# Cross-attention and expert FFN in one kernel: values laid out by partition, and the first batch's last scores, softmax and first values by halves of the queries

## The reference

```python
n = layernorm(x)                             # (8, 224, 2048)
a = einsum('bqd,bkd->bqk', n, ctx)           # scores against 750 context rows
x = x + einsum('bqk,bkd->bqd', softmax(a), ctx)
h = layernorm(x)
base = einsum('bsi,oi->bso', h, base_w) + base_b
hidden = einsum('bsi,ri->bsr', h, A)         # 64 wide
p = softmax(einsum('bsi,ei->bse', h, router_w))   # 16 experts, the best two kept
x = x + base + 0.5 * einsum('bse,bsr,eor->bso', combine(p), hidden, B)
```

## Time and profile before

| | us |
|---|---|
| median of 3 runs (1350.43 to 1354.08) | 1351.94 |
| the profiled execution, its own time | 1354.39 |
| its span, first to last instruction | 1352.6 |
| PE busy in the span | 1327.3 |
| DVE busy | 974.7 |
| ACT busy | 601.2 |
| mean granted clock of PE, share of full | 0.996 |

### The profile page before, as it was taken

How to read it: one execution, slowest core, us unless ns; L and a number is a source line. 1 busy time by engine, 2 the same in 40 slices (tenths; PEclk the granted TensorE clock), 3 DMA queues, 4 the chain that set the end, 5 groups by cost and what they waited for, 6 DMA issues and landing times.

```text
span 1352.6 us, 16784 instructions
## 1 busy us (share of the span) xinstructions
PE 1327.3 (98%) x6543; PEld 1081.0 (80%) x6543; DVE 974.7 (72%) x1254; ACT 601.2 (44%) x768; POOL 322.5 (24%) x229
## 2 busy tenths in 40 slices
PE   7799999999999999999999999999999999999998
PEld 5578788887878788887888888888788888888887
DVE  5698888889798888879475467777677555465554
ACT  3356554645546464546321367877686211111110
POOL 0003012130302112120615723354442111111110
PEclk9899999999999999999999999999999999999999
DMA  9976968878796977769657598999995977878775
GB/s 326 315 258 215 294 242 242 269 251 271 227 304 212 287 259 248 246 227 194 201 161 211 176 296 288 321 324 310 315 250 192 322 255 242 281 250 263 253 260 164
DMA packets 159359, 345.67 MB, mean 256 GB/s; under 512 B 51696, under 2 KB 68080, under 8 KB 145520
## 3 DMA queue, kind: packets, MB, share of 16 engines
q1 hardware_dynamic: 140688, 277.06, 64.5%
q0 software_dynamic: 10528, 52.85, 12.6%
q10 hardware_dynamic: 8064, 14.68, 3.1%
HBM read 260.87 MB, written 99.41 MB: 266 GB/s over the span
## 4 chain that ended last, share of the span: by engine, by line
PE 75%; DVE 12%; DMA 5%; ACT 3%; POOL 3%; issue 2%; SPq 0%; DVEq 0%; POOLq 0%; ACTq 0%
PE scores L937 12%; PE scores L939 12%; PE scores L938 12%; PE scores L906 6%; PE scores L908 6%; PE scores L907 6%; PE scores L789 4%; PE scores L791 3%; PE scores L790 3%; DVE ctxT_l L1287 3%; PE work L973 2%; PE work L974 2%; DMA y_scratch<-y_out,yrow_i 2%; DVE raw_l L1297 2%; POOL hs_scratch L1830 2%
## 5 line engine op out<-in xcount | busy, mean ns | idle before, releaser
L937 PE MATMUL scores<-w_h,a_h 128*128 128x512 f32 x896 | 352.0, 393 | 0.0
L939 PE MATMUL scores<-w_h,a_l 128*128 128x512 f32 x896 | 350.9, 392 | 0.0
L938 PE MATMUL scores<-w_l,a_h 128*128 128x512 f32 x896 | 350.6, 391 | 0.0
L1159 ACT ACTIVATE a_h<-a_in 128x512 fp32r<-128x512 f32 x148 | 83.6, 622 | 313.4 <-DMA a_in<-xT_scratch 211.3
L939 PEld LDWEIGHTS scores<-w_h,a_l 128*128 128x128 f32 x896 | 168.4, 188 | 37.5
L937 PEld LDWEIGHTS scores<-w_h,a_h 128*128 128x128 f32 x896 | 168.3, 188 | 37.5 <-DVE w_l L1584 0.3
L938 PEld LDWEIGHTS scores<-w_l,a_h 128*128 128x128 f32 x896 | 168.5, 188 | 37.1
L1593 DVE TENSOR_TENSOR a_l<-a_in,a_h 128x512 fp32r<-128x512 f32 x148 | 106.0, 763 | 115.3 <-ACT a_h L1159 111.8
L789 PE MATMUL scores<-ctxT_h,nT_h 128*112 128x494 f32 (+1 forms) x512 | 174.3, 340 | 7.8 <-DVE nT_l L1485 7.2
L1067 ACT ACTIVATE val_h<-raw_in 128x512 fp32r<-128x512 f32 x192 | 120.2, 629 | 127.6 <-PE scores L908 127.6
L791 PE MATMUL scores<-ctxT_h,nT_l 128*112 128x494 f32 (+1 forms) x512 | 171.5, 335 | 0.0
(11 more groups left out here) (168 smaller groups left out, 1936.6 us busy)
## 6 DMA issues: line engine op xcount, KB each, us to landing
ctxT_in<-in_ctxT_dram SPq DMA_DIRECT2D x63, 750.0 KB, 4.7
raw_in<-in_ctx_dram SPq DMA_DIRECT2D x32, 1280.0 KB
a_in<-xT_scratch SPq DMA_DIRECT2D x37, 1024.0 KB
w_in<-in_wT_dram SPq DMA_DIRECT2D x32, 512.0 KB, 6.7
y_add<-y_scratch SPq DMA_DIRECT2D x56, 256.0 KB, 6.2
late_y<-y_scratch SPq DMA_DIRECT2D x56, 256.0 KB, 6.0
nT_in<-in_xT_dram SPq DMA_DIRECT2D x7, 1792.0 KB, 10.1
res<-x_scratch SPq DMA_DIRECT2D x42, 256.0 KB
```

Of the source, the lines that this page charges most:

```text
L937: pe.matmul(o, ah, wh, start=(k == 0), stop=False)
L938: pe.matmul(o, ah, wl, start=False, stop=False)
L939: last = pe.matmul(o, al, wh, start=False, stop=(k == KD - 1))
```

## The change

Four things are edited together. (1) The host hands over the values as (batch, chunk, 125, 6, 512) and the kernel loads a chunk with one transfer of 125 partitions with 12 KB each; a tile is 125 rows, six of them make 750, and the last, shorter tile and the padding of `prob` are gone. (2) In batch 0, raw 1 is issued right behind raw 0, raw 2 behind `ctxT` 6, raw 3 behind `ctxT` 7. (3) In batch 0, the last two steps of the scores are reordered so that half 0 ends first; its maximum, exponentials, transposes and split come before those of half 1, and the first four value products run by halves. (4) The PSUM sides of batch 0 are swapped for that, batch 1 begins its scores with the other half, and DVE takes the first two statistics of batch 1's rows before the value products.

```diff
 def load_raw(b, c):
-    cols = slice(c * BANK, (c + 1) * BANK)
-    sp.dma_start(raw_in[:, c, 0:FULL, :],
-                 ctx[b, 0:FULL * P, cols].rearrange("(t p) d -> p t d", p=P)).then_inc(raw_loaded[c], 16)
-    sp.dma_start(raw_in[0:REST, c, FULL, :], ctx[b, FULL * P:LK, cols]).then_inc(raw_loaded[c], 16)
+    sp.dma_start(raw_in[0:KT, c, :, :], ctx[b, c]).then_inc(raw_loaded[c], 16)
...
-                    if first and j == LR + 1:
-                        load_raw(0, 1)
+                    if first and j == NPC - 2:
+                        load_raw(0, 2)
...
                     if first:
-                        load_raw(0, 2)
+                        load_raw(0, 3)
                         sp.dma_start(ar_in[:, :, :], arT).then_inc(ar_loaded, 16)
-                        load_raw(0, 3)
                         load_row(1)
...
             load_raw(0, 0)
+            load_raw(0, 1)
             one(0, "first")
...
+    def side_of(b, c):
+        return (c + 1) % 2 if b > 0 else c % 2
...
                 if stage == "first":
+                    k = KD - 2 * CP
+                    pe.wait_ge(first_ready, NPC - 1)
+                    pe.wait_ge(ctx_ready, b * NPC + NPC - 1)
+                    products(k, 0)
+                    products(k + 1, 0)
+                    products(k, 1)
                     pe.wait_ge(first_ready, NPC)
+                    pe.wait_ge(ctx_ready, b * NPC + NPC)
+                    products(k + 2, 0)
+                    products(k + 3, 0).then_inc(scores_done, 1)
+                    products(k + 1, 1).then_inc(score_step, 1)
+                    products(k + 2, 1)
+                    exps_T(stage, b, 0)
+                    products(k + 3, 1).then_inc(scores_done, 1)
+                    return
...
             def outputs_of(stage, b):
 
+                if stage == "first":
+                    pe.wait_ge(drained, job_no(stage, b, "eT", 0) + 1)
+                    for e in range(NR):
+                        if e == NR - 1:
+                            exps_T(stage, b, 1)
+                        pe.wait_ge(val_ready, b * (CH * NT) + e + 1)
+                        value_products(b, e, 0)
                 pe.wait_ge(drained, job_no(stage, b, "eT", NQ - 1) + 1)
-                for e in range(CH * NT):
+                if stage == "first":
+                    for e in range(NR):
+                        value_products(b, e, 1).then_inc(val_used, 1)
+                for e in range(NR if stage == "first" else 0, CH * NT):
...
                 row_max(b, 0)
                 if old:
                     x2T_low(2)
+                else:
+                    exps_low(0)
                 row_max(b, 1)
...
                 if old:
                     hidden_out(stage, b)
+                else:
+                    row_stats(1, 0, 2)
                 for e in range(NR, CH * NT):
                     value_low(b, e)
...
     laid["ctxT"] = ctx.transpose(0, 2, 1).reshape(nb, d // 256, 2, 128, lk).transpose(0, 1, 3, 2, 4)
+    laid["ctx_4096"] = ctx.reshape(nb, -(-lk // 128), -1, d // 512, 512).transpose(0, 3, 2, 1, 4)
```

More of the change, by code:

```diff
@@ L72, in xattn_ffn_kernel @@
     NB, LQ, D = x.shape
-    LK = ctx.shape[1]
+    LK = ctxT.shape[-1]
     E, R = bT.shape[0], bT.shape[1]
@@ L792, in products @@
                     return last
-                for j in range(NPC - 1):
+                for j in range(NPC - 1 if stage != "first" else NPC - 2):
                     if stage != "first" and j in X2T_BEFORE:
@@ L806, in scores_of @@
                     by_block = j or stage == "first"
-                    for k, q in itertools.product(ks, (1, 0)) if by_block else [(k, q) for q in (1, 0) for k in ks]:
+                    halves_first = (0, 1) if b == 1 else (1, 0)
+                    for k, q in itertools.product(ks, (1, 0)) if by_block else [(k, q) for q in halves_first for k in ks]:
                         if stage == "first" and (k, q) == (1, 1):
@@ L875, in hidden_back @@
                 last.then_inc(filled, 1)
[L877 to L886, removed]
@@ L888, in outputs_of, with exps_T @@
-            def outputs_of(stage, b):
+            def exps_T(stage, b, q):
+                pe.wait_ge(exp_done, b * NQ + q + 1)
+                take(job_no(stage, b, "eT", q))
+                slot = slot_of(stage, "eT", q)
+                for t in range(NT):
+                    at = (t // 3) * BANK + (t % 3) * QT
+                    last = pe.transpose(work[0:KT, slot, at:at + QT],
+                                        prob[:, q, t * KT:(t + 1) * KT], ident[0:QT, 0:QT])
+                last.then_inc(filled, 1)
@@ new lines, in value_products @@
+            def value_products(b, e, q):
+                c, t = e // NT, e % NT
+                out = scores[0:QT, side_of(b, c), q * BANK:(q + 1) * BANK]
+                eh, el = eT_h[0:KT, q, t, :], eT_l[0:KT, q, t, :]
+                vh, vl = val_h[0:KT, e % NR, :], raw[0:KT, c, t, :]
+                pe.matmul(out, eh, vh, start=(t == 0), stop=False)
+                pe.matmul(out, eh, vl, start=False, stop=False)
+                last = pe.matmul(out, el, vh, start=False, stop=(t == NT - 1))
+                return last
@@ L901, in outputs_of @@
                     for q in range(NQ):
[L902 to L908, removed]
+                        last = value_products(b, e, q)
                     last.then_inc(val_used, 1)
@@ L916, in one @@
                     hidden_of(stage, b, 0, HID_EARLY)
-                exps_T(stage, b)
+                if stage != "first":
+                    for q in range(NQ):
+                        exps_T(stage, b, q)
                 if stage != "first":
@@ L1037, in high @@
                 act.wait_ge(filled, job_no(stage, b, name, n) + 1)
-                src = place(stage, name, n).rearrange("p (k c) -> p k c", k=cols)[:, :, 0:width]
+                rows = out.shape[0]
+                src = place(stage, name, n)[0:rows, :].rearrange("p (k c) -> p k c", k=cols)[:, :, 0:width]
                 act.activation(out, src, ACT.Copy).then_inc(high_done, 1)
@@ L1119, in one @@
                     high(stage, b, "x2T", NX - 1, four_blocks(nT_h, NX - 1), 2, 2 * LQ)
+                three = lambda q: eT_h[0:KT, q, :, :].rearrange("p (k i) c -> p k (i c)", k=2)
+                if stage == "first":
+                    high(stage, b, "eT", 0, three(0), 2, 3 * QT)
                 exponentials(b, 1)
-                for q in range(NQ):
-                    high(stage, b, "eT", q, eT_h[:, q, :, :].rearrange("p (k i) c -> p k (i c)", k=2), 2, 3 * QT)
+                for q in range(1 if stage == "first" else 0, NQ):
+                    high(stage, b, "eT", q, three(q), 2, 3 * QT)
                 for e in range(NR, CH * NT):
@@ L1281, in low @@
                 dve.wait_ge(high_done, act_no(stage, b, name, n) + 1)
-                src = place(stage, name, n).rearrange("p (k c) -> p k c", k=cols)[:, :, 0:width]
+                rows = low_part.shape[0]
+                src = place(stage, name, n)[0:rows, :].rearrange("p (k c) -> p k c", k=cols)[:, :, 0:width]
                 dve.tensor_tensor(low_part, src, as_f32(high_part), ALU.subtract).then_inc(drained, 1)
@@ L1536, in one, with exps_low @@
                         value_low(b, 2 * (j - (NPC - 2)) + 1)
+                def exps_low(q):
+                    three = lambda tile: tile[0:KT, q, :, :].rearrange("p (k i) c -> p k (i c)", k=2)
+                    low(stage, b, "eT", q, three(eT_h), three(eT_l), 2, 3 * QT)
                 row_max(b, 0)
@@ L1542, in one @@
                     x2T_low(NX - 1)
-                for q in range(NQ):
-                    three = lambda tile: tile[:, q, :, :].rearrange("p (k i) c -> p k (i c)", k=2)
-                    low(stage, b, "eT", q, three(eT_h), three(eT_l), 2, 3 * QT)
+                for q in range(0 if old else 1, NQ):
+                    exps_low(q)
                 if old:
                     hidden_out(stage, b)
+                else:
+                    row_stats(1, 0, 2)
                 for e in range(NR, CH * NT):
@@ L1550, in one @@
                     c, t = e // NT, e % NT
-                    if new and e in STATS_AT:
+                    if new and e in STATS_AT and (old or e > STATS_AT[0]):
                         n = 2 * STATS_AT.index(e)
```

29 lines of the change are left out of this document (11 added, 18 removed).

## The result

The changed kernel takes **1523.96 us** (median of 5 runs, 1521.48 to 1528.04) against 1352.98 for the kernel before (5 runs, 1350.43 to 1357.36): ratio 1.1264, interval 1.1235 to 1.1293. It is slower, as forecast, but by 171 us where 109 were forecast, and outside the range. The profiled execution took 1523.96 us, its span 1522.2 us, 169.6 more than before; the mean granted clock fell from 0.996 to 0.945.

The account below looks back on a forecast made before the run. PE, busy 98% of the span, was taken as the bound, losing time wherever loads queued on five DMA engines idle it: 16 + 7.4 + 66 + 20 = 109 us on 1352 gives 1461 us, range 1365 to 1510.

Parts of the forecast that it names:

- The number of engines: Raw loads: the largest number up to 16 that divides the partitions, so 125 partitions get 5 engines with 25 each.
- The clock term: After the stalls of batches 1 to 7, PE restarts at 1.2 GHz: 2.9 us each, 20 us in all, bounds 0 and 25.
- B: Rival for raw loads: five engines, but other ones from load to load, so no backlog; 1352 us, chance 0.04.
- C: Rival: the same five engines, but later batches have more slack, so only batch 0 loses; 1368 us, chance 0.06.
- A: Rival: the 125 partitions spread over all sixteen engines, stops of batch 0 go and halves win; 1345 us, chance 0.08.
- D: Rival for raw loads: fewer engines than five, one in the worst case; over 1900 us, chance 0.02.
- the size of a raw load: 1.536 MB on five engines at 26.4 GB/s each: 11.6 us for every raw load, bounds 3.6 and 20 us.
- upper bound of 20 us: A raw load's longest time, with 26.4 GB/s replaced by the 238 GB/s rate seen with a row load.
- Batch 0: Queued raw loads delay the last score block; first value product at 74, not 57.96: 16 us lost, bounds 14 and 21.
- Batches 2 to 7: 17.3 us of work ahead of `ctxT` 4 stalls PE 11.0 us in each of six batches: 66 us.
- the formula (less 6.3): Before the fifth score step, B us of queued work ahead of `ctxT` 4 cost PE B - 6.3 us.
- Batch 1: `ctxT` 4 finds 13.7 us of work ahead: a 7.4 us stall, with 2.9 us of clock loss counted separately.

Follow-up runs that it names:

- e1: The whole change, but each raw load fills 128 partitions (three repeated, unused rows), against the kernel before: 1351.81 us, ratio 0.9989.
- e6: The kernel before with the layout alone, loaded by 128 partitions (three repeated rows unused): 1351.87 us, ratio 0.9994 to the kernel before.
- e7: The kernel before with the layout by 128 partitions and the new order of batch 0's loads: 1352.53 us, ratio 0.999.
- e4: The whole change with 125 partitions, but values left in row order, so six 2 KB runs a partition: 1514.72 us, ratio 1.118 to the kernel before.
- e2: The whole change, but each raw load split into two transfers of 112 and 13 partitions: 1365.2 us, ratio 1.0098 to the kernel before.
- e8: The whole change with 125-partition raw loads, but issued by ScalarE on its own queue: 1560.67 us, ratio 1.1502 to the kernel before.

## Why the prediction was wrong in size and right in kind

**Right.** The number of engines: the queue of all SP issues counts 20704 packets fewer than before (first line before, second after),

```profile
q1 hardware_dynamic: 140688, 277.06, 64.5%
...
q1 hardware_dynamic: 119984, 277.06, 58.7%
```

which is 32 chunks x 647: by the prediction's working a chunk had 640 + 16 and 110 + 11 = 777 packets, and now has 130, 125 of data and 5 that close it. The same five each time: raw 0 and raw 1, issued together, ran one after the other. Nearly undisturbed, a load took 12.3 us from first to last packet (743.8 to 756.1), at a share of 0.30 where it was alone, against the 11.6 forecast. The place was right: PE stops ahead of the fifth score step in each batch, ACT behind the DMA. The clock term was right in kind and somewhat too large: the granted clock was 0.50 (the lower level) when PE began again, and of the 20.1 us that batches 2 to 6 lost in the mean the stop is 17.8, which leaves 2.3 for the clock against 2.9 forecast. The two restart windows above give about as much for one batch: 3.54 us at half the clock and 4 us at 0.89 lose some 2.2. The FFN kept its length. The early `row_stats` was not free as forecast: PE waited 1.8 us behind it once. Rivals B and C fell with the period of 94.5 to 98.0 us, A and D with the five closing packets; that a load on all engines, by 128 partitions, would save the kernel is what e1 shows.

**The step that failed** is the size of a raw load: "I take 11.6, since longer runs per partition should not be slower than a `ctxT` load's, and that ran at full rate." The number nearly held for a load alone and was used for loads beside others: 16.5 us each in batch 0's first pair, 19 for raw 2 there, 15.0 to 15.6 in a middle batch's pair, about halfway to the upper bound of 20 us. That bound rests on 238 GB/s "with a row load among the transfers"; the packet records show the row load alone there. The prediction met the effect ("the row load is slower than its bytes"), put it down to the row load, and still took 4.3 us for one, where batch 0's first took 7.1 in the kernel before (21.6 to 28.7). So it had the sign that a load of fewer than 128 partitions can be slower than its engines' full rate, and did not use it for the raw load.

What follows from it, by the prediction's own steps:
- *Batch 0*: 33 us for raw 0 and 1 where 23.2 stood, 19 for raw 2 where 11.6 stood. That is 17.2 us more, and the first value product came at 92.08, 18 after the forecast 74. Behind it PE idled 2.9 us more (1.8 behind `raw_l`, 1.0 behind `eT_l`), so the 16 became 37.0.
- *Batches 2 to 7*: the pair took 30.1 to 31.2 us and not 23.2. Put into the same working, the backlog at `ctxT` 4 is 17.3 + 6.9 = 24.2 to 17.3 + 8.0 = 25.3, and the formula (less 6.3) gives a stop of 17.9 to 19.0; measured 18.1 in the mean of these six. Their stops sum to 108.6 us where 66 stood: 42.6 of the 62 us that were missing.
- *Batch 1*: 12.8 against 7.4 + 2.9, of which the stop is 11.9 against 7.4.

The range failed with it: its upper end allowed 13 us for each raw load, not the 20 that stood as a bound, and it had no case in which a load is fast alone and slow beside others.

**Rival A's price** was too good as well: with sixteen engines the new orders were to give 1345, and e1 has 1351.81. PE's waits for `nT_l` in batch 0 go from 7.2 to 5.7 us only. e6, with the old order, has 5.7 as well, and e7 5.3, so the order of the loads took away next to nothing of the stops; that the bytes ahead of the last `ctxT` set them is not shown.

**What slows the packets** is shown as far as this: a load of 125 partitions on five engines and loads of 128 partitions slow one another (460 to 870 ns, 229 to 430); a load of 112, or of 112 + 13, is slow on sixteen engines even alone (492 and 714 ns); loads that all have 128 partitions keep their median times (e1); so does the load of 125 beside stores; and the length of the packets is not the reason (e4). Why, no run shows: the packet records don't tell which engine wrote which partition. The Trainium skill offers a place: bandwidth depends on how many of SBUF's 16 ports the partitions reach (SBUF — State Buffer, section on door 1, the DMA port swizzle), and in a 128-partition transfer each engine writes one port of its own (DMA: Bandwidth & Descriptors, section on the descriptor swizzle). If other counts of rows are dealt out as runs of neighbours, several engines could meet on one port. e1 against e2 agrees with that, but no trace here shows a port or how the rows are dealt out, so it stays an argued cause.

## What to carry to other kernels

Before a layout with fewer than 128 partitions is chosen, work out how many DMA engines the transfer gets, and try padding it to 128 rows: three unused rows in 128 were worth some 170 us here. All sixteen engines are not enough by themselves: 112 + 13 rows still cost 1.0%. A transfer's duration alone is not its duration in the kernel; price it from a window in which the same neighbours run. And another queue did not take away the backlog on a few engines here (e8), since every transfer with a share on those engines waited for it on either queue.

## What was not expected of the hardware

- Sixteen busy engines can move half of what they move elsewhere: 210 GB/s at a share of 0.94, against 422 at full rate. The share of the DMA engines alone doesn't tell that transfers run well; the GB/s beside it does.
- The slowdown is mutual: the 128-partition `ctxT` load went from 229 to 430 ns a packet beside the load on five engines, and by the sum of their times mostly on other engines than those five. From 424 to 431 us, 152 packets of `ctxT` at 443 ns in the mean make nearly ten engines' time and 42 of the raw loads at 856 ns make five's.
- A load can slow itself with all sixteen engines at work: 112 partitions of 8 KB took 492 ns a packet alone (before, 22 to 28 us), 311 when five engines were left. Padding to 128 was tried for the raw loads only; whether it would help the row loads was not tried.
- Two queues shared the engines packet by packet, although one had 12 KB packets and the other 512 B: a store waited 460 ns of raw load for each packet, and an issue of 2.70 us became one of 46.42.
